# A Mixture-of-Experts layer pair on one core: each row scatter of the first routing waits until the scatter two in front of it has landed

## The reference, cut to what matters

```python
x = x + _L0_attn_ref(_layernorm(x, axis=-1), ...)
x = x + _L0_ffn_ref(_layernorm(x, axis=-1), gate_w, w1, b1, w2, b2)

# inside _L0_ffn_ref (h is x after the layer norm, flattened to 8192 rows)
logits = x @ gate_w.T                       # 14 experts
probs = jax.nn.softmax(logits, axis=-1)
top2_p, top2_i = jax.lax.top_k(probs, 2)
w = top2_p / jnp.maximum(top2_p.sum(-1, keepdims=True), 1e-10)
hh = gelu(jnp.einsum('nd,edf->nef', x, w1) + b1)
all_out = jnp.einsum('nef,efd->ned', hh, w2) + b2
moe_out = w[:, 0:1] * out0 + w[:, 1:2] * out1   # out0, out1: the rows of the two best experts
result = jnp.clip(x + moe_out, -100.0, 100.0)
```

## Time and profile before

| | |
|---|---|
| time, median of 3 runs | 2156.17 us (2154.11 to 2160.58) |
| time of the profiled execution | 2157.69 us |
| its span, first to last instruction | 2156.0 us |
| mean granted TensorE clock | 0.883 |
| POOL busy over the span | 1447.5 us (67%) |
| the 128 scatters of line 1215 | 126.4 us busy, 43.4 us idle ahead of them |

### The profile page before, as it was taken

How to read it: one execution, slowest core, us unless ns; L and a number is a source line. 1 busy time by engine, 2 the same in 40 slices (tenths; PEclk the granted TensorE clock), 3 DMA queues, 4 the chain that set the end, 5 groups by cost and what they waited for, 6 DMA issues and landing times. The chain is left out here.

```text
span 2156.0 us, 58282 instructions
## 1 busy us (share of the span) xinstructions
PE 1659.2 (77%) x18607; PEld 1179.1 (55%) x18607; DVE 1406.7 (65%) x3640; ACT 1170.8 (54%) x2283; POOL 1447.5 (67%) x1159
## 2 busy tenths in 40 slices
PE   7978999999999999988601999377777775100997
PEld 3434777777777767757601888144444443000997
DVE  5757888888888888846601443288888886710553
ACT  4635888888888888876400554134444444021443
POOL 0005999999999999983775333788888873065565
PEclk9987999999999999999755999699989897555999
DMA  4753222222222222224321333300000000132232
GB/s 145 251 195 111 64 69 66 71 64 71 66 67 72 63 67 69 67 61 149 104 78 49 124 127 116 118 21 19 21 19 18 18 15 3 42 122 93 91 103 61
DMA packets 158123, 169.72 MB, mean 79 GB/s; under 512 B 39522, under 2 KB 124393, under 8 KB 157961
## 3 DMA queue, kind: packets, MB, share of 16 engines
q1 hardware_dynamic: 143128, 137.02, 20.7%
q0 software_dynamic: 13824, 29.43, 4.3%
q10 hardware_dynamic: 1008, 0.92, 0.1%
HBM read 93.57 MB, written 73.97 MB: 78 GB/s over the span
## 5 line engine op out<-in xcount | busy, mean ns | idle before, releaser
L776 DVE TENSOR_REDUCE halfmax<-p_m 128x1 f32<-128x512 f32 x1024 | 634.5, 677 | 123.8 <-PE p_m L644 123.5
L763 ACT ACTIVATE probs<-p_s,ESCALE 128x512 f32<-128x512 f32 x1024 | 635.4, 689 | 25.4 <-PE p_s L674 11.5
L674 PE MATMUL p_s<-qa,ka 98*32 98x512 f16 x4096 | 497.4, 383 | 8.9 <-DMA qa<-max_lo 6.1
L644 PE MATMUL p_m<-ka,qa 96*32 96x512 f16 x4096 | 484.1, 390 | 12.7 <-DMA vh<-v 11.9
L593 POOL TENSOR_TENSOR sum_p<-sum_p,probs 128x1024 f32<-128x1024 f32 x192 | 456.4, 2377 | 11.0
L681 PE MATMUL p_o<-probs,vh 128*32 128x256 f32 x4096 | 366.8, 381 | 0.3 <-ACT probs L763 0.3
L1633 PE MATMUL ln_p_cum<-ln_kv,c_tri 128*128 128x512 f32 (+1 forms) x384 | 169.7, 587 | 91.1 <-POOL ln_kv L1577 91.1
L644 PEld LDWEIGHTS p_m<-ka,qa 96*32 96x32 f16 x4096 | 160.7, 97 | 114.1 <-DVE halfmax L776 31.5
L1290 ACT ACTIVATE e_h<-e_p_h,e_w 128x256 f32<-128x256 f32 x316 | 126.1, 473 | 172.9 <-PE e_p_h L1269 172.6
L674 PEld LDWEIGHTS p_s<-qa,ka 98*32 98x32 f16 x4096 | 174.2, 96 | 78.2 <-ACT probs L763 12.3
L681 PEld LDWEIGHTS p_o<-probs,vh 128*32 128x32 f32 x4096 | 188.5, 111 | 43.7 <-issue 1.8
(11 more groups left out here) (293 smaller groups left out, 2825.4 us busy)
## 6 DMA issues: line engine op xcount, KB each, us to landing
e_xb<-xs SPq DMA_DIRECT2D x40, 257.0 KB, 2.6
e_xb<-xs SPq DMA_DIRECT2D x78, 128.0 KB, 2.0
ys<-e_y SPq DMA_DIRECT2D x78, 128.0 KB, 1.9
v<-pj_v SPq DMA_DIRECT2D x8, 1024.0 KB, 4.9
qa<-q SPq DMA_DIRECT2D x64, 128.0 KB, 2.7
ka<-k SPq DMA_DIRECT2D x64, 128.0 KB, 2.7
vh<-v SPq DMA_DIRECT2D x64, 128.0 KB, 2.2
o<-ot SPq DMA_DIRECT2D x64, 128.0 KB
```

Source lines behind the costliest of these rows:

```text
L644: mm = nc.tensor.matmul(max_bank(s, n)[j * DH0:(j + 1) * DH0, :], qa[s][0:KA, (n // 2) * P + j * DH0:(n // 2) * P + (j + 1) * DH0], ka[s][ ...
L674: mm = nc.tensor.matmul(score_bank(s, k, h)[j * DH0:(j + 1) * DH0, :], ka[s][:, cols], qa[s][:, q], start=True, stop=True, tile_position=( ...
L763: nc.scalar.activation(probs[k][:, h * HALF:(h + 1) * HALF], score_bank(s, k, h)[:, :], ACT.Exp, scale=ESCALE[:, 0:1]).then_inc(probs_d, 1)
L776: nc.vector.reduce_max(halfmax[s % 2][:, n // 2, n % 2:n % 2 + 1], max_bank(s, n)[:, :], AX.X).then_inc(max_read, 1)
```

## The change

A scatter now waits until the one two in front of it has landed. The semaphores are dealt out by choice `k` and no longer by sequence, so that scatter n and scatter n-2 share one. A wait is put ahead of every scatter but the first two of a sequence. Ahead of the cast of every sequence but the first, POOL now waits for all scatters of all sequences before it, on both semaphores.

```diff
             for b in range(B):
                 pool.wait_ge(places, b + 1)
-                if b >= 2:
-                    pool.wait_ge(rows_out[b % 2], b // 2 * ST * 2 * 16)
+                if b:
+                    for k in range(2):
+                        pool.wait_ge(rows_out[k], b * ST * 16)
                 nc.gpsimd.tensor_copy(slot[b % 2][:, :], tabs["slotf"][:, b * ST * 2:(b + 1) * ST * 2]).then_inc(slot_d, 1)
                 apart(pool, slot_d, b + 1, passed)
                 for i in range(2):
                     for t in range(G):
                         for k in range(2):
                             n = (i * G + t) * 2 + k
+                            if i or t:
+                                pool.wait_ge(rows_out[k], (b * ST + i * G + t) * 16)
                             pool.indirect_dma_start(xs[:, :], bass.IndirectOffsetOnAxis(ap=slot[b % 2][:, n:n + 1], axis=0),
-                                                    group_of(XN, 2 * b + i)[:, t, :], None).then_inc(rows_out[b % 2], 16)
-            for i in range(2):
-                pool.wait_ge(rows_out[i], B // 2 * ST * 2 * 16)
+                                                    group_of(XN, 2 * b + i)[:, t, :], None).then_inc(rows_out[k], 16)
+            for k in range(2):
+                pool.wait_ge(rows_out[k], B * ST * 16)
```

## The result

The changed kernel takes 2181.57 us in the median of 4 runs (2178.63 to 2186.86). The kernel before took 2157.97 us beside it (2154.11 to 2160.58). The ratio is 1.0114, with a 95% interval of 1.0087 to 1.014, so the change costs 1.1%. The profiled execution took 2180.75 us with a span of 2179.0 us, against 2157.69 and 2156.0 before: 23.1 us more.

A forecast was written before the change was run, and what follows sets the result against it. POOL's fixed-pace row of scatters was taken to bound stage `route2`. Costs of 9.5 + 1 + 9 + 1 = 20.5 us on the profiled 2157.7 gave 2178.2, forecast as a median of 2177 us, range 2165 to 2208.

The forecast's parts named there:

- The end of the stage: End of `route2`: next stage's first load starts 4.84 us behind POOL's last scatter, so each microsecond later costs the kernel one.
- Between sequences: POOL's cast waits for the last scatter's landing, seven times: 3.3 us for 1.98, 1.3 to 1.4 each, 9.5 us.
- Inside a sequence: Quiet scatters: landing 2.24 plus restart 0.25 to 0.30 us about equals today's 2.52 spacing; cost taken as 1 us.
- The loaded part: First two sequences, beside SP's transfers: landings of 3.0 us make two scatters take 3.28 instead of 2.52; 9 us.
- the zeros: SP's writes of zeros at 1076 us, 7 us long, too short to cost more than 1 us.
- The long restart: Rival: scatter preparation starts only after the wait, restart 0.81 us, two scatters 3.05 us; +47 us, 2204; chance 0.33.
- Landings of 2.2 us with fewer under way: Rival, loaded part: the wait itself brings landings to 2.2 us, its 9 us fall away; +11 us, 2167; chance 0.09.
- The shrinking gap: Rival: gap between scatters falls from 0.30 to 0.14 us, giving 2169; chance 0.04 shared with waits that do nothing.
- the waits do nothing: Rival: all waits met on arrival, time stays at 2156; chance 0.04 shared with the shrinking gap.
- no change: Whole kernel: closing chance 0.04 that the time stays within 0.3% of the kernel before.
- a gain: Whole kernel: closing chance 0.02 that it gets faster by over 0.3%.

The follow-up runs named there:

- spaced_wide: Kernel before plus three small fills of an unused tile behind each scatter, no new wait: 2168.1 us, ratio 1.0044.
- first_four: Changed kernel with its waits only up to the cast of the fifth sequence, then those of the kernel before: 2180.74 us, ratio 1.0113 to the kernel before.
- one_in_front: Changed kernel, but each scatter waits for the one directly in front instead of two in front: 2332.48 us, ratio 1.0595 to the kernel before.
- after_third: Changed kernel measured once more, unedited, beside a kernel before of about 2158 us: 2180.15 us, ratio 1.0115.
- before_again: Kernel before, unedited, measured again in a group where the kernel before took 2200.68 us: 2203.6 us, ratio 1.0014.
- separate_wait: Changed kernel with each inner wait in an instruction of its own ahead of the scatter: 2214.17 us, ratio 1.0055 to a kernel before of 2200.68 us.

## Why the prediction was right, point by point

**The end of the stage is POOL's last scatter.** Right. The next stage's load stands 4.84 us behind it before and after, and `spaced_wide` moves the stage's end through POOL's pace alone.

**Between sequences: forecast 1.3 to 1.4 us each, 9.5 in all.** Measured 3.40 - 1.98 = 1.42 us each in the quiet part, 9.9 in all. The step that was slightly off is the start of the cast behind the landing. It begins 1103.93 - 1101.54 = 2.39 us behind the start of the scatter that it waits for, 0.15 us behind the landing at 2.24 (0.154 us, four times, in `first_four`, where these landings are on record); I had taken 0.06 from the earlier trace rows, where the cast waits for DVE and not for a landing.

**Inside a sequence: forecast a restart of 0.25 to 0.30 us, and a cost of 1 us in all.** Right: 0.27 us, measured by `one_in_front`, and a cost of nothing. The quiet sequences are 18.95 us long before and after, and `first_four` gains nothing there by leaving the waits out. It is a narrow thing: 2.24 + 0.27 = 2.51 where 2.52 stood, and in the unrounded times of the changed kernel the quiet scatters start 0.28 to 0.30 us behind the landing, 0.02 to 0.03 more than they need. No row before gave the restart; it was chosen near the lower of rows from 0.06 to 0.88 us, and that it fell on the free side by so little is in part luck. With the wait in an instruction of its own the same waits cost 26 us. The rule of the Trainium skill that I had weighed against it ("Perfetto Trace Analysis", section "DMA Instruction — SWDGE (GPSIMD)": the transfer is decoded, pushed into a queue, and waits for its semaphores there) agrees with both measurements: 0.27 us when the transfer carries the wait, 0.78 us when it stands behind one. What the 0.5 us between the two are made of, no trace here shows.

**The loaded part: forecast 9 us, and 1 for the zeros.** The mechanism was right and the size a little short. The first two sequences grew by 7.2 and 2.9 us. The distance between them is 6.09 us, 2.7 more than in the quiet part, because the cast met a landing that came late. This I had left out: I had priced the wait of the cast everywhere by the quiet landing of 2.2 us. The zeros cost the change nothing, where I had 1 us. In their time some of POOL's own instructions are drawn out, in both kernels: scatters of 1.17, 1.90 and 1.09 us in the fourth sequence of the kernel before, a cast of 0.74 us instead of 0.20 and a scatter of 1.34 us in the changed one. So the distance behind the third sequence is 3.97 us, 0.6 more, and the fourth sequence is 0.9 us shorter; no late landing is in either. In all 7.2 + 2.9 + 2.7 + 0.6 - 0.9 = 12.5 us, and with 9.9 us between sequences 22.4 of the 22.5 measured, where I had 20.5. Where the late landings fall differs from one execution to the next: in `after_third` all seven distances are 3.40 us, the first two sequences are 24.5 and 24.9 us long, and the lengths have grown by 12.2 us in all. That it is SP's traffic which makes landings late was argued and not tested. Most late ones fall where SP's queue works, but in the kernel before one at 1046 us takes 3.3 us while that queue is empty.

**The rivals.** The long restart falls by `one_in_front`. Landings of 2.2 us with fewer under way fall by the row of 1000 to 1021 us: 3.2 us in the median and 4.6 at most, with at most two under way, against 3.0 and 4.4, and by `one_in_front`, where only one is under way and landings of 4.9 us still occur. A small gain isn't excluded: `first_four`, with the same waits as the changed kernel and all landings on record, has 2.6 us in the median for its 13 scatters of this time. The shrinking gap falls too, the gap is 0.30 us before and after. That the waits do nothing is true of those inside the quiet sequences, and not of the others.

**The total.** 2181.57 us against a forecast of 2177: of the 4.6 us, 2.0 are the terms above (22.5 against 20.5), 0.6 the first scatter's later start less the shorter remainder (2.6 - 2.0), and 2.0 the median's distance from the profiled execution: I had put it 1.2 us below (1.5, before rounding to 2177), and it lies 0.8 above. By terms, the waits between sequences were 9.9 for 9.5, the quiet inner waits 0 for 1, the loaded part with the zeros 12.5 for 10. One slip doesn't touch the forecast: the closing chances for no change (0.04) and for a gain (0.02) come to 0.06, where the rivals leave 0.02 for both.

**What I had not foreseen** is that the sign depends on a condition of the machine. Where the kernel before takes 2158 us the change costs 1.1%, twice measured. Where it takes 2201 us the change gains 0.5%. What makes this condition stays open. It isn't the program, since `before_again` is the same one, and it isn't the chip alone. Shown is what goes on in it: signals of PE that arrive up to 14 us late, when POOL pauses; transposes on PE that start 1.4 us apart in some stretches; sequences that are placed every 25 us instead of 10.5; and that the places keep nearly their old pace in the two kernels whose scatters come 1.5 or 2.5 us apart to the end. Whether it is their pace itself was not told apart from other things that a wait for a landing changes, since no kernel that is slowed without such a wait was measured in this condition. Nor is it shown why a running row of scatters holds these signals up.

## What to carry to other kernels

A wait on an engine that sets the end of a stage costs nothing as long as the event it waits for, plus the restart, comes inside the spacing that the engine keeps anyway. Measure both and subtract: a releaser's name in the trace is no price, only a gap that grew is. Put the wait into the transfer itself, not ahead of it, and price a wait separately where other traffic makes the landings late, also at the seams between loops. Measure the kernel before again beside every group of runs: here the same change costs 1.1% in one group and gains 0.5% in another.

## What the runs showed of the hardware that was not expected

- An indirect scatter on POOL that carries its own wait starts 0.265 to 0.268 us behind the landing it waits for (`one_in_front`). Behind a separate wait it starts 0.78 us behind the landing (`separate_wait`, 3.02 us for two scatters less a landing of 2.24). A cast on POOL starts 0.15 us behind a landing, and 0.06 us behind DVE's end.
- The gap of 0.30 us between two scatters takes up other work of POOL: a fill of 0.14 us costs nothing there (step 1.27 us), three fills of 0.22 us together cost 0.08 us (step 1.345 us).
- There is a condition of the machine in which the same program takes 2201 us instead of 2158. Between the profiled executions it is 47 us, of which 35 lie between the first and the last scatter (204.3 us against 169.4) and 13 behind it (1000.3 against 987.7). PE's semaphore increments for its transposes come up to 14 us behind the end of the instruction there (0.01 us otherwise), and the copies that wait for them start about 4 us behind the start of the last scatter before POOL pauses. PE also starts transposes 1.4 us apart in some stretches, with no releaser in the trace. The changed kernel's stage is 191.5 us in it and 191.9 outside it.
